# Mamba block and mixture of experts: which token groups the first expert slots wait for, and who writes the padding rows

## What is computed

```python
h = _layernorm(x) * (1 + ca) + sa
x = x + ga * attn(h)          # Mamba block: 512 channels, 16 states, a scan over 1024 steps
h = _layernorm(x) * (1 + cb) + sb
x = x + gb * ffn(h)           # mixture of experts
# ffn: 8 experts of 256 -> 512 -> 256, each token takes its best 2
gate_logits = einsum('bsd,de->bse', x, gate_kernel)
top_k_weights, top_k_indices = top_k(gate_logits, 2)     # softmax over the two
out = sum over the two of weight * (silu(x @ w0[e]) * (x @ w1[e])) @ wo[e]
```

## Time and profile before

| | |
|---|---|
| median of three runs | 869.93 us (866.11 to 870.88) |
| the profiled execution | 869.48 us |
| its span in the trace | 867.7 us |
| PE busy over the span | 718.0 us (83%) |
| DVE, POOL, ACT busy | 646.8, 520.7, 329.2 us |
| mean granted TensorE clock | 0.969 of full speed |

### The profile page before, as it was taken

One profiled execution on the slowest core, in us unless ns is written; L12 is line 12 of the kernel. 1 busy time (PEld: TensorE's weight loads), 2 busy tenths in 40 slices (PEclk: granted clock), 3 DMA queues, 4 the chain that ended last, 5 costly groups with the idle time before them and its releaser, 6 DMA issues.

```text
span 867.7 us, 10126 instructions
## 1 busy us (share of the span) xinstructions
PE 718.0 (83%) x2245; PEld 357.5 (41%) x2246; DVE 646.8 (75%) x881; ACT 329.2 (38%) x364; POOL 520.7 (60%) x274
## 2 busy tenths in 40 slices
PE   5899998678787877877776877994679999999994
PEld 3444343222232322322222322784346666666662
DVE  4488899999999999999999999574434444445442
ACT  1786956456454445435444444101111111111110
POOL 1013235999989899998989999356632222222222
PEclk9999999999999999999999999995699999999997
DMA  9345647757667666666779786492322222322220
GB/s 287 104 135 163 212 170 179 206 151 191 173 159 212 147 188 183 177 178 162 199 183 240 180 210 169 170 387 101 120 60 49 45 36 45 48 42 40 45 29 1
DMA packets 59700, 125.28 MB, mean 144 GB/s; under 512 B 11098, under 2 KB 31002, under 8 KB 59548
## 3 DMA queue, kind: packets, MB, share of 16 engines
q1 hardware_dynamic: 48644, 115.05, 48.6%
q0 software_dynamic: 7536, 9.55, 6.0%
q10 hardware_dynamic: 3496, 0.41, 0.3%
HBM read 98.08 MB, written 23.63 MB: 140 GB/s over the span
## 4 chain that ended last, share of the span: by engine, by line
PE 37%; DVE 31%; issue 10%; POOL 10%; ACT 6%; DMA 2%; another core or an unknown queue 1%; DVEq 1%; ACTq 0%; SPq 0%; POOLq 0%
DVE pool L1138 20%; PE PS L723 16%; PE PS L739 8%; POOL pool L1407 7%; ACT PS L889 6%; PE PS L506 4%; PE PS L627 3%; PE PS L611 2%; DVE pool L1126 2%; PE PS L731 2%; POOL spread L1427 2%; DVE pool L1072 2%; DVE pool L1070 1%; DVE Y L1081 1%
## 5 line engine op out<-in xcount | busy, mean ns | idle before, releaser
L1407 POOL TENSOR_TENSOR pool<-pool,hT 128x1024 f32<-128x1024 f32 x128 | 298.5, 2358 | 17.6 <-PE PS L611 17.6
L611 PE MATMUL PS<-pool,ident 128*128 128x512 f32 x512 | 245.7, 602 | 29.8 <-POOL pool L1407 28.5
L889 ACT ACTIVATE PS<-pool,negA 128x1024 f32 (+1 forms) x128 | 143.1, 1118 | 192.6 <-DVE pool L1138 192.6
L1138 DVE TENSOR_TENSOR_SCAN pool<-PS,pool 128x1024 f32<-128x1024 f32 x96 | 215.7, 2275 | 0.0
L1476 POOL DMA_INDIRECT out<-uT,ptab x39 | 60.6, 1554 | 165.4 <-DVE uT L1353 163.0
L611 PEld LDWEIGHTS PS<-pool,ident 128*128 128x128 f32 x512 | 92.7, 189 | 129.4 <-issue 70.2
L723 PE MATMUL PS<-pool,uT 128*128 (+1 forms) x312 | 144.9, 608 | 0.8 <-issue 0.8
L593 PE MATMUL PS<-pool 96*128 96x512 bf16 x256 | 77.1, 382 | 63.4 <-DVE pool L1126 60.2
L1126 DVE TENSOR_TENSOR pool<-PS,pool 128x1024 f32<-128x1024 f32 x96 | 117.6, 1225 | 11.2 <-DVE pool L1138 0.9
L1327 DVE TENSOR_TENSOR uT<-uT,PS 128x512 f32<-128x512 f32 x39 | 26.9, 689 | 97.9 <-PE PS L723 82.3
L1427 POOL TENSOR_TENSOR spread<-spread,pool 128x1024 f32<-128x1024 f32 x32 | 75.4, 2357 | 16.3 <-ACT spread L895 16.3
(11 more groups left out here) (176 smaller groups left out, 737.0 us busy)
## 6 DMA issues: line engine op xcount, KB each, us to landing
hT<-C_scratch SPq DMA_DIRECT2D x128, 512.0 KB, 5.2
pool<-in_w SPq DMA_DIRECT2D x16, 512.0 KB, 7.0
uT<-expert_in_scratch SPq DMA_DIRECT2D x39, 130.5 KB
Y<-Y SPq DMA_DIRECT2D x32, 128.0 KB, 2.4
C_scratch<-Y SPq DMA_DIRECT2D x8, 512.0 KB, 2.6
pool<-du_scratch SPq DMA_DIRECT2D x8, 512.0 KB, 6.3
Y<-in_wo SPq DMA_DIRECT2D x8, 512.0 KB
x_tok<-in_x SPq DMA_DIRECT2D x4, 512.0 KB, 8.7
```

Source lines behind the costliest of these rows:

```text
L611: m = pe.matmul(PS[:, 6 + half, :], ident[:, :], prod[:, k % PR, HF * half:HF * half + HF], start=False, stop=k == DS - 1)
L889: act.activation(pair(2 * (k % 2)).unsqueeze(1), delta[:, bass.ds(g2 * 2 + r, 1), :], ACT.Exp, scale=decay[:, bass.ds(g2 * (2 * DS) + n, 1 ...
L1138: dve.tensor_tensor_scan(hst[:, k % HR, :], pair(2 * (k % 2)), driven, 0.0, ALU.mult, ALU.add).then_inc(scan_done, 1)
L1407: gp.tensor_tensor(prod[:, k % PR, :], hst[:, k % HR, :], crep[k % RC], ALU.mult).then_inc(prod_done, 1)
```

## The change

SP waits for groups 0 and 1 only before slots 0 to 7, and the mark `late` is found after group 1 (fewer than 128 rows by then). The tails start at row max(count, 128) and are written from ScalarE's queue, two after each of the first four silus of its loop, whose first two rounds are written out; each takes a register load of `tail_row` and a plain DMA. The first 128 rows of each region and the eight empty blocks are zeroed by 16 DMAs of SP's queue, one after every second load of C in the scan's last two chunks; POOL waits for them before its first send. Slots from 8 on wait for the tails (`tails_out`).

```diff
@@ -94,7 +94,7 @@
         iota_s = sb("iota_s", [P, NS])
         tri_f = sb("tri_f", [P, P])
         zrow = sb("zrow", [P, XW])
-        tail_row = sb("tail_row", [P, NE], U32)
+        tail_row = sb("tail_row", [P, NE], I32)
         ready = sb("ready", [P, NE], I32)
         since = sb("since", [P, 1])
         Dcol = sb("Dcol", [P, NB * CH])
@@ -208,7 +208,6 @@
         fall = take(NE)
         reach = take(NE * NX).rearrange("p (j s) -> p j s", s=NX)
         rf = take(NX)
-        own_row = take(NE)
         late = take(NE)
 
         wo_sb = Y[:, :].rearrange("p (e k n) -> p e k n", e=NE, k=KM)
@@ -258,7 +257,8 @@
         x2_out, noted, meta_done, gsel_done, yo_free, added = (sem(n) for n in ("x2_out", "noted", "meta_done", "gsel_done", "yo_free", "added"))
         col_in = sem("col_in")
         ident_by_in, wdt_in, wz_in, placed_w = (sem(n) for n in ("ident_by_in", "wdt_in", "wz_in", "placed_w"))
-        placed, tails_known, ready_known, arrived = sem("placed"), sem("tails_known"), sem("ready_known"), sem("arrived")
+        placed, tails_known, ready_known, arrived, tails_out = (
+            sem(n) for n in ("placed", "tails_known", "ready_known", "arrived", "tails_out"))
 
 
         def by_place(rows):
@@ -375,8 +375,10 @@
 
             sp.sem_inc(stk_free, 1)
             sp.wait_ge(zero_rows, 4)
-            sp.dma_start(xs_dram[NE * RT:XR, :].rearrange("(n p) c -> p n c", p=P),
-                         zrow[:, :].unsqueeze(1).broadcast_to([P, 8, XW])).then_inc(xs_zeroed, 16)
+            def emptied(n):
+                first = n * RT if n < NE else NE * RT + (n - NE) * P
+                sp.dma_start(xs_dram[first:first + P, :], zrow[:, :]).then_inc(xs_zeroed, 16)
+
             sp.sem_inc(prod_done, RC)
 
             def w0_of(e):
@@ -392,6 +394,8 @@
                         sp.dma_start(crep[k % RC],
                                      C_dram.rearrange("(h s) n -> h s n", s=DS)[bass.ds((g2 * 2 + r) * HC, HC), k, :]
                                      .unsqueeze(0).broadcast_to([DS, HC, L])).then_inc(crep_in[k % RC], 16)
+                        if last and k % 2:
+                            emptied(r * NE + k // 2)
                         if last and k in (3, 7, 11):
                             w0_of(3 * r + k // 4)
                         if k == DS // 2 and not (last and r == 1):
@@ -427,7 +431,7 @@
             sp.wait_ge(o_mm, NT)
             sp.wait_ge(ready_known, 1)
             sp.sem_inc(arrived, 1)
-            for q in range(NQ - 1):
+            for q in range(NQ // 2):
                 sp.wait_ge(sent[q], 16 * 2 * TQ)
             for e in range(NE):
                 if e >= 2:
@@ -437,7 +441,7 @@
                 sp.wait_ge(arrived, needed)
                 rows_in(e * RT, e % 2)
             sp.wait_ge(c_over, 1)
-            sp.wait_ge(xs_zeroed, 16)
+            sp.wait_ge(tails_out, 16 * NE)
             sp.wait_ge(arrived, 2)
 
             def row_of(slot):
@@ -675,7 +679,7 @@
 
             def ranks(q):
                 pe.wait_ge(picked, q + 1)
-                for i in range(TQ + (q >= NQ - 2)):
+                for i in range(TQ + (q in (NQ // 2 - 1, NQ - 1))):
                     to = PS[:, 6 + q % 2, P + NE * i:P + NE * i + NE]
                     parts = [(ones, ohs[:, TQ * q + j, :]) for j in range(i)]
                     if q:
@@ -971,7 +975,18 @@
             take_rows(0, 0)
             take_rows(0, 1)
             silu_h(0, 0)
-            with act.Fori(0, SPAIRS) as s2:
+            def tail(e):
+                first = act.value_load(tail_row[0:1, e:e + 1], min_val=0, max_val=XR - P)
+                act.dma_start(xs_dram[bass.ds(first, P), :], zrow[:, :]).then_inc(tails_out, 16)
+
+            act.wait_ge(tails_known, 1)
+            for s2 in range(2):
+                for r in range(2):
+                    take_rows(s2 + 1, r)
+                    silu_h(s2 + r, 1 - r)
+                    tail(4 * s2 + 2 * r)
+                    tail(4 * s2 + 2 * r + 1)
+            with act.Fori(2, SPAIRS) as s2:
                 for r in range(2):
                     take_rows(s2 + 1, r)
                     silu_h(s2 + r, 1 - r)
@@ -1170,8 +1185,6 @@
                 step(dve.tensor_scalar(e_rows, iota8[:, :], float(RT), None, ALU.mult))
                 step(dve.tensor_copy(ef[:, 0:NE], iota8[:, :]))
                 step(dve.tensor_copy(etab[:, 0:NE], iota8[:, :]))
-                settled()
-                step(dve.tensor_scalar(own_row, e_rows, since[:, :], float(T), ALU.subtract, ALU.add))
 
             def added_y(t):
                 dve.wait_ge(o_mm, t + 1)
@@ -1252,7 +1265,7 @@
                 step(dve.tensor_copy(posu[:, :, tiles], posf[:, q]))
                 settled()
                 dve.sem_inc(placed, 1)
-                if q == NQ - 2:
+                if q == NQ // 2 - 1:
                     step(dve.tensor_scalar(late, PS[:, 6 + q % 2, P + TQ * NE:P + TQ * NE + NE], float(P), 1.0,
                                            ALU.is_lt, ALU.add))
                     settled()
@@ -1293,7 +1306,7 @@
 
             step(dve.tensor_copy(cnt, PS[:, 6 + (NQ - 1) % 2, P + TQ * NE:P + TQ * NE + NE]))
             settled()
-            dve.tensor_tensor(tail_row[:, :], cnt, own_row, ALU.add).then_inc(tails_known, 1)
+            dve.scalar_tensor_tensor(tail_row[:, :], cnt, float(P), e_rows, ALU.max, ALU.add).then_inc(tails_known, 1)
             step(dve.tensor_scalar(cnti, cnt, -1.0, 0.0, ALU.add, ALU.max))
             dve.wait_ge(tails_known, 1)
             settled()
@@ -1450,6 +1463,7 @@
             rstd_of(0)
             rstd_of(1)
             gp.wait_ge(noted, 2)
+            gp.wait_ge(xs_zeroed, 16 * 2 * NE)
             for q in range(NQ):
                 gp.wait_ge(placed, q + 1)
                 if q < NQ - 2:
@@ -1459,11 +1473,8 @@
                 else:
                     send(q, slice(0, 2 * TQ))
 
-            gp.wait_ge(tails_known, 1)
-            for e in range(NE):
-                gp.indirect_dma_start(out=xs_dram, out_offset=bass.IndirectOffsetOnAxis(ap=tail_row[:, e:e + 1], axis=0),
-                                      in_=zrow[:, :], in_offset=None).then_inc(sent[NQ - 1], 16)
-            gp.wait_ge(sent[NQ - 1], 16 * (2 * TQ + NE))
+            for q in range(NQ // 2, NQ):
+                gp.wait_ge(sent[q], 16 * 2 * TQ)
             gp.sem_inc(arrived, 1)
 
             gp.wait_ge(x2_out, 16 * 4)
```

## The result

Over ten runs each the kernel before takes 869.81 us (866.11 to 872.03) and the changed one 863.21 us (862.43 to 864.95). The ratio is 0.993, with a 95% interval from 0.9913 to 0.9947: 6.6 us, or 0.8%, faster. It had the direction right and the size too large. The measured time lies in the range of 857.5 to 868.5, and 0.2 us outside the range that the forecast gave its own first case (857.5 to 863). Its largest term, the 6.05 us for the tails, came out nearly in full, but part of that was luck: the edit that moves the tails also takes a second wait off the path, and the forecast did not have that wait in it. In the experiments, on other chips, that wait is the whole worth of the tails' move.

What follows compares the result with a forecast made beforehand. Steady slots were taken as bound by PE, so gains had to come from PE's idle between routing and the first slots. 2.42 + 0.70 + 6.05 = 9.2 us off 869.48 gave 860.3 us, range 857.5 to 868.5.

Steps and rivals of the forecast that it cites:

- first case: All gains arrive together: 860.3 us, own range 857.5 to 863, chance 0.61.
- the 6.05 us for the tails: Slot 1: moving tails off POOL removes PE's late signal, 4.17 us idle plus the half-speed part behind it; 6.05 us.
- The early read: First slots: loading after groups 0 and 1 starts PE 4.4 us earlier; slot 2's load leaves 2.4 us of it.
- The 0.70 "issue": Slot 0: PE's wait for DVE's product disappears because DVE has it long before PE asks; 0.7 us gained.
- Slots 0 and 1 are loaded near 590 us.: Sign of being right: first two slots load once the last tile's projection is in, 20 us before PE is free.
- POOL's first work for a slot comes after them, so that in itself is worth nothing.: End of POOL's eight tails: its slot work starts only behind them, and that order alone was priced at nothing.
- The rival with code fetching: Slot 1's delay stays, from PE's program or other traffic: 3.1 us gained, 866.4 us, or 868.3 with half speed; chance 0.29.
- Tails on ACT: Between silu and next copy: two register loads and issues, 1.7 to 2.5 us, hidden in 3.06 us of idling.
- Empty rows: Sixteen zeroing DMAs behind the scan's loads of C cost nothing, upper bound 21 us; sign: POOL idles at most 17.6 us.
- The sum: Whole kernel: 2.42 + 0.70 + 6.05 = 9.2 us below the profiled 869.48 us, giving 860.3 us.

Runs made afterwards that it cites:

- r1: The kernel before, unedited, profiled again on a later chip; one execution took 861.12 us.
- r2: The changed kernel, unedited, on a later chip; 854.27 us against 859.49 for the kernel before, ratio 0.993.
- e5: The kernel before, with SP waiting for groups 0 and 1 alone and POOL granting result buffers before its wait for tails; 854.22 us, ratio 0.9919.
- e1: The kernel before, with SP waiting for groups 0 and 1 alone and the mark after group 1, tails still on POOL; 861.70 us, ratio 1.0027.
- e7: The kernel before, with only POOL's grant of the result buffers moved ahead of its wait for the tails; 860.25 us, ratio 1.0007.
- e9: The kernel before, with SP waiting for groups 0 and 1, POOL's grant early, DVE's notes behind the last places, tails on POOL; 853.19 us, ratio 0.9932.
- e4: The kernel before, with POOL's tails issued two behind each add of slots 0 to 3 and `arrived` after slot 4's add; 860.02 us, ratio 1.0008.
- e3: The changed kernel, with all 16 DMAs of empty rows before the scan and none in it; 853.92 us, ratio 0.9934.
- e6: The changed kernel, with DVE's notes of slots 0 and 1 moved ahead of the last group's picks; 854.51 us, ratio 0.9934.
- e8: The changed kernel, with DVE's notes of slots 0 and 1 between last places and tables, and POOL's grant early; 852.46 us, ratio 0.9919.

## Why the forecast was right, and where it was wrong

**The early read.** Its mechanism held: PE's first turn 0.23 us after the ranks, and slot 2's load next. The rule for its size held too (when PE would have come to slot 2, less when slot 2 lands). In the later profiles the turn of slot 2 starts at 621.69 in r1 and at 616.81 in r2: 5.0 us earlier from P, and 6.0 at hidden of slot 1. In the first pair of profiles it was sized at 3.1 with the "issue" of slot 0 and measured 1.69 (the table): slot 0's last note, which frees the buffer for slot 2, starts at 622.48 - 547.87 = 74.61 us from P, where the forecast had 618.42 - 544.44 - 0.36 = 73.62. The 0.70 "issue" did go. Not in the sum: hidden of slot 1 runs behind the new idle of 2.04 us and takes 4.57 instead of 3.70, at a granted clock of 0.79. I had this as a loss only in the rival. The same place in r2: 1.99 us of idling, then 4.86 us for the product; in e5: 1.78 us, then 3.70 at a granted clock of 1.00.

**"Slots 0 and 1 are loaded near 590 us."** Wrong by 14: SP's wait ends at 602.75 and the loads go at 603.81 and 606.85. POOL forms the scale of group 3's rows between group 1's third and fourth send (`rstd_of`), and I read the landings without it. It costs nothing, as PE comes for them at 616.

**"POOL's first work for a slot comes after them, so that in itself is worth nothing."** This is the step of the mechanism that failed. I looked at the add and not at the grant that stands in the same place of POOL's program. DVE's first scaled result needs the grant, in order, with the next slot's work behind it. The earlier trace rows had the number: the last tail ends at 633.54, and the grant, which waits for its landing, can't come before. The line of the grant in that first profile (ns of one, first and last start):

```profile
L1470 POOLq EVENT_SEMAPHORE  x1: 17/17/17, 635.2 to 635.2; - x1
```

DVE's scaled result can start some 0.25 us behind it (0.24 in e1). PE's modelled end of hidden of slot 1 was 629.22. So even with no late signal DVE would have stood at the grant for some 4 us. I had looked for who waits for the tails' rows, and the answer, slots from 8 on, was right; who waits behind them I did not ask.

**The 6.05 us for the late signal.** In the profile it came out nearly as forecast: 5.53 - 1.69 = 3.84 at hidden of slot 2 and 1.89 more at slot 3. The forecast gave it to the tails' being on POOL. On the three later chips that is not borne out: of the 12 profiles there, six have the indirect tails on POOL (r1, e1, e5, e7 and e9 in a row, e4 two by two), and none has a row "remote" between 548 and 642 us.

For the first measurement it stays open. Both its profiles have such rows, before seven at five places and after four at three, so late signals are not bound to the tails. But nearly all of them end while POOL issues a row of indirect DMAs, sends as well as tails, or about 1 us behind the last. In the kernel before, two places besides that of the earlier trace rows:

```profile
586.86 0.96 POOL L1447 DMA_INDIRECT expert_in_scratch<-pool,posu  x1 [0.30 <-issue]
...
589.07 0.66 ACT L946 ACTIVATE hT<-PS 128x256 f32<-128x256 f32 x2 [10.53 <-remote]
...
597.25 0.96 POOL L1447 DMA_INDIRECT expert_in_scratch<-pool,posu  x1 [0.30 <-issue]
599.14 0.19 DVE L1244 TENSOR_TENSOR hT<-PS,hT 128x32 f32<-128x32 f32 x1 [2.19 <-remote]
```

and in the changed one, the first of these rows at the end of a row of sends, the last inside one:

```profile
589.78 0.96 POOL L1460 DMA_INDIRECT expert_in_scratch<-pool,posu  x1 [0.30 <-issue]
591.80 0.42 DVE L1191 TENSOR_TENSOR x_tok<-PS,x_tok 128x256 f32<-128x256 f32 x1 [1.59 <-remote]
...
610.45 0.38 ACT L950 ACTIVATE hT<-PS 128x256 f32<-128x256 f32 x1 [3.18 <-remote]
```

The signals come 1.25, 0.93 and 1.06 us behind the end of such a row, and 1.05 us behind it in the earlier trace rows. The last one delays group 3's logits. In slot 1 of the changed kernel POOL's last send ends at 627.46 and the signal, due near 631.8, is on time. That is what one would see if POOL's indirect DMAs held up PE's signals in that measurement; then the tails' move did take a delay away there, and the forecast's reason holds for it. Against it: inside the same rows other signals of PE come on time (DVE's L1204 at 593.76 in the kernel before is released by PE), and the same rows of DMAs on the later chips delay none. Two profiles can't settle it.

What remains of the term is the gate: in e1 hidden of slot 3 starts 5.52 us after POOL's L1470 (636.22 - 630.70), and by that 635.2 + 5.5 = 640.7 is what the grant alone would have allowed in the first profile, where 644.01 was seen and 638.0 forecast without the delay. So of the 6.05 some 3.3 were the signal's, whatever its cause, and 2.7 the gate's. That split is worked out, not measured.

**The rival with code fetching.** The packet on queue 8 is there in the changed kernel as well, in the stretch from 626 to 632 us, and PE's signal in slot 1 is on time:

```profile
q8 instruction: 1, 0.02, 1.0%
```

It is also there in r1, the kernel before unedited, from 622 to 624 us, with the signal on time (the percentage is of that shorter window):

```profile
q8 instruction: 1, 0.02, 4.4%
```

All 14 profiles have one such packet on queue 8 between 610 and 630 us, and in 13 of them no signal in slot 1 is late. So the packet is no sign of a delay. By the rule of the Trainium skill (Runtime: NRT & Kernel Launch, Instruction fetch mechanics) a taken branch to code outside the blocks held waits for that code; such a stall would belong to PE's own program and would have stayed after the change. No run here shows one. The rival's other half, that the delay is not the tails', fits the later chips and is open for the first measurement; its price of 3.1 us left out the gate as well.

**Tails on ACT.** Hidden, as forecast. From the silu's end at 630.74 to the second issue's end at 632.55 the register loads and issues take 1.8 us of the gap (forecast 1.7); the next copy still waits for PE, by the same 3.06 us as in the earlier trace rows. ACT's issues, and the copy behind them:

```profile
631.08 1.47 ACTq L980 DMA_DIRECT2D expert_in_scratch<-zrow  x2
633.80 0.39 ACT L966 ACTIVATE uT<-PS 128x256 f32<-128x256 f32 x1 [3.06 <-PE PS L714]
```

An issue took 338 to 384 ns, at the lower end of my bounds. I had expected the idle to fall to 1.3; it did not, since queue instructions are not counted as busy.

**Empty rows.** Nothing that can be measured, as forecast. The page after, beside the earlier trace rows. POOL's idle before the products is 18.9 us, above the 17.6 that I had set as the sign; but it is 19.1 to 22.4 in the six other profiles of the kernel before and its variants, and 19.0 in e3, so that sign was set within the scatter. PE is still what releases POOL, and e3 says the same of the time:

```profile
L1420 POOL TENSOR_TENSOR pool<-pool,hT 128x1024 f32<-128x1024 f32 x128 | 298.9, 2365 | 18.9 <-PE PS L615 18.5
...
hT<-C_scratch SPq DMA_DIRECT2D x128, 512.0 KB, 5.3
```

**The sum.** Forecast 9.2 us, measured 7.42 from P to slot 3 in one pair of profiles and 6.6 in the medians (5.2 and 4.9 on two later chips). Of the 1.8 between the first two, 1.4 are slot 2's notes and loads, 0.9 the lower clock in hidden of slot 1, and 0.5 came back in small idles of slot 1 that I had not counted (1.4 + 0.9 - 0.5 = 1.8). The step from 7.42 to the 6.6 of the medians is within what single executions differ by.

## What to carry to other kernels

When a wait is shortened, list every semaphore that the late engine gives from behind the same point of its program, grants of buffers as well as data: here one `sem_inc` behind a wait for landings was worth as much as moving eight DMAs to another engine. Two gates in series each test as worthless alone, so a part that "does nothing" by itself is no evidence until it was tried with the others open. Notes that let the next load start should stand at the first point of their engine's program where their data has surely landed, and not before: e6 had them too early and gained nothing; e8 had them later and took PE's wait away, though its 1.85 us are not clear of noise.

## What the runs showed of the hardware

- One and the same kernel took 869.8 us in the first measurement and 859.3 to 859.5 us on three chips later, with ratios to the changed kernel that agree within their intervals. In the profiles the difference lies between the scan's last product and hidden of slot 3: 99.6 against 88.0 us before, 92.2 against 83.2 after. Late signals account for a part of it. What causes them stays open.
- An indirect DMA of 128 rows holds POOL for 0.96 us, and 0.30 us pass before the next: eight in a row are 9.8 us (first profile: 623.72 to 633.54), and the last lands 2.6 us after its start (2.62 in e1). On ACT a plain DMA of the same rows with its row number in a register is issued in 0.34 to 0.38 us, and costs about 0.9 us with the register's load.
- Single profiles of the scan scatter: its last product starts between 544.4 and 548.1 us over 14 profiles, more than half of what the whole change brought. Short stretches have to be compared from a common event.
